# Sharing six PSUM banks as three for row scores and three for column scores, handed on tile by tile

## The reference, cut to what matters

```python
scores = jnp.einsum('bkgsd,bktd->bkgst', qh, kh) / scale
weights = jax.nn.softmax(scores, axis=-1)
out = jnp.einsum('bkgst,bktd->bkgsd', weights, vh)
...
x = x + jnp.tanh(g_xattn[0]) * xattn(_layernorm(x), ctx_512, ctx_512)
x = x + jnp.tanh(g_ffn[0]) * ffn(_layernorm(x), w_gate, w_up, w_down)
```

## Time and profile before

| | before |
|---|---|
| median of 3 runs | 472.99 us (472.53 to 473.21) |
| profiled execution | 472.9 us |
| its span in the trace | 471.1 us |
| TensorE busy in the span | 457.5 us (97%) |
| VectorE, ScalarE, GpSimd busy | 387.8, 291.7, 217.5 us |
| attention, about | 20 to 174 us |

### The profile page before, as it was taken

The page is one execution under the profiler, slowest core; times in us unless marked ns, Lnnn a source line. Parts: engine busy times, 40 slices in busy tenths (PEclk is TensorE's granted clock), DMA queues, the critical chain, the costliest instruction groups (busy, mean ns, idle before and its releaser), DMA issues.

```text
span 471.1 us, 8996 instructions
## 1 busy us (share of the span) xinstructions
PE 457.5 (97%) x3108; PEld 299.2 (64%) x3128; DVE 387.8 (82%) x715; ACT 291.7 (62%) x464; POOL 217.5 (46%) x335
## 2 busy tenths in 40 slices
PE   9999999999999989989999999999999999999997
PEld 8665656666566534468944479864469874479664
DVE  5879988788877659859998967999885999889891
ACT  3488886677778688877647417653616663657460
POOL 4355556989898464655006734203926300930000
PEclk9999999999999999999999999999999999999999
DMA  7999120121014041000100651100361110152086
GB/s 233 323 349 352 36 52 11 24 58 25 13 25 111 13 162 40 2 0 13 24 11 3 111 140 27 22 11 0 69 154 46 24 24 0 33 91 57 1 141 217
DMA packets 68183, 35.90 MB, mean 76 GB/s; under 512 B 50288, under 2 KB 62960, under 8 KB 68144
## 3 DMA queue, kind: packets, MB, share of 16 engines
q1 hardware_dynamic: 67408, 34.48, 28.8%
q10 hardware_dynamic: 736, 0.92, 0.6%
HBM read 19.26 MB, written 4.19 MB: 50 GB/s over the span
## 4 chain that ended last, share of the span: by engine, by line
PE 78%; DVE 9%; ACT 5%; issue 5%; DMA 1%; POOL 1%; DVEq 0%; SPq 0%; POOLq 0%; ACTq 0%
PE ps L872 16%; PE ps L623 10%; PE ps L926 9%; PE ps L949 9%; PE ps L605 8%; PE ps L666 6%; PE ps L683 4%; PE ps L938 2%; PE ps L940 2%; PE ps L815 2%; PE ps L585 2%; PE ps L725 2%; DVE y_split L1440 2%; ACT wst L1067 2%; PE ps L631 1%
## 5 line engine op out<-in xcount | busy, mean ns | idle before, releaser
L872 PE MATMUL ps<-wst 128*128 128x512 bf16 x499 | 111.7, 379 | 3.3 <-DVE wst L1460 2.1
L1297 DVE TENSOR_REDUCE reg<-ps 128x4 f32<-128x512 f32 x128 | 81.8, 683 | 24.9 <-PE ps L623 23.3
L872 PEld LDWEIGHTS ps<-wst 128*128 128x128 bf16 x512 | 49.2, 98 | 62.1 <-DVE wst L1460 4.1
L623 PE MATMUL ps<-reg 32*128 32x256 f32 x512 | 86.8, 400 | 0.5 <-DVE reg L1297 0.2
L569 POOL TENSOR_TENSOR reg_rest<-reg_rest,z_sc 128x1024 f32<-128x1024 f32 x24 | 47.4, 2010 | 84.7 <-DVE z_sc L1502 84.7
L1029 ACT ACTIVATE reg<-ps 128x1024 f32<-128x1024 f32 x64 | 65.6, 1025 | 33.0 <-PE ps L631 32.9
L1160 ACT ACTIVATE wst<-wst 128x512 f32<-128x512 f32 x64 | 40.0, 626 | 51.4 <-DVE wst L1460 51.0
L926 PE MATMUL ps<-had_f,wst 128*128 128x128 f32 x512 | 67.1, 276 | 1.1 <-DVE wst L1465 1.1
L926 PEld LDWEIGHTS ps<-had_f,wst 128*128 128x128 f32 x512 | 64.0, 191 | 4.4 <-DVE wst L1465 1.8
L605 PE MATMUL ps<-reg 32*128 32x512 f32 x232 | 65.2, 639 | 0.0
L623 PEld LDWEIGHTS ps<-reg 32*128 32x128 f32 x512 | 58.7, 184 | 6.0 <-issue 1.0
(11 more groups left out here) (172 smaller groups left out, 739.2 us busy)
## 6 DMA issues: line engine op xcount, KB each, us to landing
wst<-in_w SPq DMA_DIRECT2D x16, 512.0 KB, 8.6
reg<-in_w SPq DMA_DIRECT2D x8, 512.0 KB, 5.6
out<-x_all SPq DMA_DIRECT2D x16, 256.0 KB, 2.1
x_all<-in_x SPq DMA_DIRECT2D x3, 1024.0 KB, 9.5
reg<-in_v SPq DMA_DIRECT2D x4, 256.0 KB, 4.2
reg<-in_k_t SPq DMA_DIRECT2D x28, 32.0 KB, 2.7
x_all<-in_x ACTq DMA_DIRECT2D x1, 512.0 KB, 6.6
reg_rest<-reg SPq DMA_TRANSPOSE x20, 3.1
```

Of the source, the lines that this page charges most:

```text
L623: last = pe.matmul(ps[:, row_banks(r) + m, 256 * g:256 * g + 256], q_t[n % 4][strip(i), P * h:P * h + P], kpad[n // CHUNK % 2][strip(i), n ...
L872: last = pe.matmul(ps[:, banks[ob % n], :], tern_gu[:, ob // 2, m, j, P * (ob % 2):P * (ob % 2) + P], q1_t[:, j, :], start=(j == 0), stop= ...
L1297: dve.tensor_reduce(neg_max[n % 2][:, g:g + 2, i + m, :], ps[:, row_banks(r) + m, :].rearrange("p (g a t) -> p g a t", g=2, a=2), AX_X, AL ...
```

## The change

Rows get banks 0 to 2 and columns banks 3 to 5, each used in rotation by single tiles. A row tile waits for the third tile before it to be reduced, in place of the second; only in the first quarter on three banks (r = 7) does it wait as before. A column tile waits for the exponential of the third tile before it. `cols_done` and `exp_done` count tiles, not quarters: each mask product increments, and each exponential of 512 columns. All waits on these counts, on SP, TensorE and ScalarE, are restated in tiles. The six lone quarters keep their pairs of banks and their exponentials of 1,024 columns; their first pair waits for all exponentials before it. The first two column quarters both wait for 12 maxima, where the first waited for 10.

```diff
-        C_BANKS = 2
+        ROW_BANKS, COL_BANKS = 3, 3
+        TILES = 2 * QUARTERS
...
-        def column_bank(c):
+        def column_bank(c, m):
             if c < LONE:
-                return C_BANKS + 2 * (c % 2)
-            return (2, 0, 4)[(c - LONE) % 3]
-        def row_banks(r):
-            return 2 * (r % 3) if r < LEAD else 0
+                return ROW_BANKS + (2 * c + m) % COL_BANKS
+            return (2, 0, 4)[(c - LONE) % 3] + m
+        def row_bank(r, m):
+            if r < LEAD:
+                return 2 * (r % 3) + m
+            return (2 * (r - LEAD) + m) % ROW_BANKS
...
                 if exists(b):
-                    reach(pe, sem("exp_done"), c - 1)
                     if c < 2:
-                        pe.wait_ge(sem("max_done"), 2 * (5 + c))
+                        pe.wait_ge(sem("max_done"), 2 * 6)
                     for m, i in enumerate(own):
-                        pe.matmul(ps[:, bank + m, :], ...
+                        reach(pe, sem("exp_done"), 2 * c + m - COL_BANKS + 1)
+                        pe.matmul(ps[:, column_bank(c, m), :], ...
...
-                    past = r - 1 if r >= LEAD else r - 3
                     for m, i in enumerate(other):
-                        reach(pe, sem("max_done"), 2 * past + 1 + m)
+                        if r >= LEAD + 1:
+                            reach(pe, sem("max_done"), 2 * r + m - ROW_BANKS + 1)
+                        elif r == LEAD:
+                            pe.wait_ge(sem("max_done"), 2 * r + m - 1)
+                        else:
+                            reach(pe, sem("max_done"), 2 * (r - 3) + 1 + m)
...
                     for m, i in enumerate(own):
-                        last = pe.matmul(ps[:, bank + m, :], sel[strip(i), a, :], ...)
-                    last.then_inc(sem("cols_done"), 1)
+                        pe.matmul(ps[:, column_bank(c, m), :], sel[strip(i), a, :], ...
+                                  ).then_inc(sem("cols_done"), 1)
...
                 for k in range(2):
-                    pe.wait_ge(sem("exp_done"), c + k - (1 if c + k == LONE else 2))
+                    pe.wait_ge(sem("exp_done"), 2 * (c + k) - (0 if c + k == LONE else 4))
...
-                act.wait_ge(sem("cols_done"), c + 1)
                 reach(act, sem("pv_done"), 2 * n + j // 2 - 1)
-                bank = column_bank(c)
-                act.activation(probs[:, 2 * j:2 * j + 2, :], ps[:, bank:bank + 2, :], ACT.Exp,
-                               scale=D ** -0.5).then_inc(sem("exp_done"), 1)
+                if c < LONE:
+                    for m in range(2):
+                        act.wait_ge(sem("cols_done"), 2 * c + m + 1)
+                        act.activation(probs[:, 2 * j + m, :], ps[:, column_bank(c, m), :], ACT.Exp,
+                                       scale=D ** -0.5).then_inc(sem("exp_done"), 1)
+                else:
+                    act.wait_ge(sem("cols_done"), 2 * c + 2)
+                    bank = column_bank(c, 0)
+                    act.activation(probs[:, 2 * j:2 * j + 2, :], ps[:, bank:bank + 2, :], ACT.Exp,
+                                   scale=D ** -0.5).then_inc(sem("exp_done"), 2)
```

More of the change, by code:

```diff
@@ L313, in turn_maxima @@
                 sp.wait_ge(sem("ms"), 5 * n + 5)
-                sp.wait_ge(sem("cols_done"), QUARTERS * (n - 1))
+                sp.wait_ge(sem("cols_done"), TILES * (n - 1))
                 sp.dma_start_transpose(m_t[n % 2].rearrange("p (g q) -> p g q", g=G), m_parts).then_inc(sem(f"m_in{n % 2}"), 16)
             def more_keys(c):
-                sp.wait_ge(sem("cols_done"), QUARTERS * CHUNK * (c - 1))
+                sp.wait_ge(sem("cols_done"), TILES * CHUNK * (c - 1))
                 load_keys(c)
@@ L327, in _ @@
                 if b == 12:
-                    sp.wait_ge(sem("cols_done"), 3 * CHUNK * QUARTERS)
+                    sp.wait_ge(sem("cols_done"), 3 * CHUNK * TILES)
                     sp.wait_ge(sem("pv_done"), 2 * 3 * CHUNK)
@@ L335, in _ @@
                     turn_maxima(b + 1)
-            sp.wait_ge(sem("cols_done"), NB * QUARTERS)
+            sp.wait_ge(sem("cols_done"), NB * TILES)
             sp.wait_ge(sem("v_set"), NB // CHUNK)
@@ L598, in quarter @@
                 own, other = (2 * (j % 2), 2 * (j % 2) + 1), (2 * (k % 2), 2 * (k % 2) + 1)
-                a, bank = j // 2, column_bank(c)
+                a = j // 2
                 if exists(b):
-                    reach(pe, sem("exp_done"), c - 1)
                     if c < 2:
-                        pe.wait_ge(sem("max_done"), 2 * (5 + c))
+                        pe.wait_ge(sem("max_done"), 2 * 6)
                     for m, i in enumerate(own):
-                        pe.matmul(ps[:, bank + m, :], kpad[b // CHUNK % 2][strip(i), b % CHUNK, a, :], q_t[b % 4][strip(i), :],
+                        reach(pe, sem("exp_done"), 2 * c + m - COL_BANKS + 1)
+                        pe.matmul(ps[:, column_bank(c, m), :], kpad[b // CHUNK % 2][strip(i), b % CHUNK, a, :], q_t[b % 4][strip(i), :],
                                   start=True, stop=False)
@@ L610, in quarter @@
                         for m, i in enumerate(own):
-                            last = pe.matmul(ps[:, bank + m, :], sel[strip(i), a, :], m_t[0][strip(i), :], start=False, stop=True)
-                        last.then_inc(sem("cols_done"), 1)
+                            pe.matmul(ps[:, column_bank(c, m), :], sel[strip(i), a, :], m_t[0][strip(i), :], start=False, stop=True
+                                      ).then_inc(sem("cols_done"), 1)
                 if exists(n):
@@ L617, in quarter @@
                             pe.wait_ge(sem(f"k_in{n // CHUNK % 2}"), 16 * NKV * (n // CHUNK // 2 + 1))
-                    past = r - 1 if r >= LEAD else r - 3
                     for m, i in enumerate(other):
-                        reach(pe, sem("max_done"), 2 * past + 1 + m)
+                        if r >= LEAD + 1:
[4 more added lines that the diff above has]
+                            reach(pe, sem("max_done"), 2 * (r - 3) + 1 + m)
                         for g in range(2):
                             h = 2 * (k // 2) + g
-                            last = pe.matmul(ps[:, row_banks(r) + m, 256 * g:256 * g + 256], q_t[n % 4][strip(i), P * h:P * h + P],
+                            last = pe.matmul(ps[:, row_bank(r, m), 256 * g:256 * g + 256], q_t[n % 4][strip(i), P * h:P * h + P],
                                              kpad[n // CHUNK % 2][strip(i), n % CHUNK, :, :].rearrange("p a t -> p (a t)"),
@@ L630, in quarter @@
                     for m, i in enumerate(own):
-                        last = pe.matmul(ps[:, bank + m, :], sel[strip(i), a, :], m_t[b % 2][strip(i), :], start=False, stop=True)
-                    last.then_inc(sem("cols_done"), 1)
+                        pe.matmul(ps[:, column_bank(c, m), :], sel[strip(i), a, :], m_t[b % 2][strip(i), :], start=False, stop=True
+                                  ).then_inc(sem("cols_done"), 1)
             def column_pair(b, j):
@@ L646, in column_pair @@
                     for m, i in enumerate((2 * k, 2 * k + 1)):
-                        last = pe.matmul(ps[:, column_bank(c + k) + m, :], sel[strip(i), a, :], m_t[b % 2][strip(i), :],
+                        last = pe.matmul(ps[:, column_bank(c + k, m), :], sel[strip(i), a, :], m_t[b % 2][strip(i), :],
                                          start=False, stop=True)
-                    last.then_inc(sem("cols_done"), 1)
+                    last.then_inc(sem("cols_done"), 2)
             def weigh(n, kvh):
@@ L656, in weigh @@
                     pe.wait_ge(sem("v_set"), n // CHUNK + 1)
-                pe.wait_ge(sem("exp_done"), QUARTERS * n + 2 * kvh + 2)
+                pe.wait_ge(sem("exp_done"), TILES * n + 4 * kvh + 4)
                 reach(pe, sem("oev_done"), 2 * n + kvh)
@@ L889, in gate_up @@
                         turn_out(NB - 1, 1)
-                        pe.wait_ge(sem("exp_done"), QUARTERS * NB)
+                        pe.wait_ge(sem("exp_done"), TILES * NB)
                         early_groups()
@@ L977, in project_last @@
                     product(LAST_TO[tb], tb, q2_last, 0, NC).then_inc(sem("d_done"), 1)
-            pe.wait_ge(sem("exp_done"), QUARTERS * NB - 1)
+            pe.wait_ge(sem("exp_done"), TILES * NB - 2)
             pe.wait_ge(sem("max_done"), 2 * QUARTERS * NB)
@@ L1042, in copy_max @@
                 act.wait_ge(sem("tm_done"), n + 1)
-                reach(act, sem("cols_done"), QUARTERS * (n - 1))
+                reach(act, sem("cols_done"), TILES * (n - 1))
                 act.copy(m_t[n % 2], M_BANK).then_inc(sem("mt_done"), 1)
@@ L1049, in copy_queries @@
                 act.wait_ge(sem("tq_done"), n + 1)
-                reach(act, sem("cols_done"), QUARTERS * (n - 3))
+                reach(act, sem("cols_done"), TILES * (n - 3))
                 act.copy(q_t[n % 4], O_BANK).then_inc(sem("qt_done"), 1)
```

4 lines of the change are left out of this document (2 added, 2 removed).

## The result

The changed kernel takes 469.98 us, the median of 20 runs (469.62 to 477.1), against 472.45 us for the kernel before in the same series (472.12 to 480.7, also 20 runs): a ratio of 0.9964, interval 0.9948 to 0.9979. A second series, with twelve runs of it, gave 470.07 us and 0.993 (0.9905 to 0.9956). The forecast was 469.5 us. The profile read here is therefore that of the second series: span 468.1 us, 469.93 us in all, where before had 471.1 and 472.9.

What follows compares the result with a forecast made beforehand. The bound was taken as TensorE's order, stretched by waits for VectorE. Gains 0.5 + 0.7 + 0.4 + 0.8 + 1.6 less 0.6 lost make 3.4 us, giving 469.5 us; range 466.6 to 472.4.

Steps and rivals of the forecast that it cites:

- The bound: Attention, 20 to 166 us: TensorE's order, stretched by waits for VectorE that its busy share hides; ceiling 11.5 us.
- The exponential's wait: Ten quarters, mostly first ones from step 5: second column product 0.16 us late, so 1.75 becomes about 1.43.
- Steps 1 to 4: After step 1's first quarter: ceiling 1.2 us less three second-quarter stalls of 0.17, 0.7 gained.
- The start: Step 0 and the first quarter of step 1: 0.5 us gained, between 0 and the ceiling 2.5.
- Step 5: Step 5 of the attention: 0.6 us less one exponential wait of 0.16, 0.4 gained.
- Steps 11 to 14: After the first quarter of step 11: 2.2 us less four exponential waits of 0.16, 1.6 gained.
- The cap: Steps 6 to 11: GpSimd, with little idle time, limits the gain to 0.8 of 5.0 us.
- Rival 1: Steps 6 to 11: GpSimd caps nothing, 3.9 us gained in place of 0.8, total 466.4 us; chance 0.1.
- The lone pair: End of attention: first lone pair newly waits for the last quarter's exponential, 0.6 us lost.
- Rival 2: Exponential halves without overlap take most of the gain back; 1 to 2 us remains, 471.5 us; chance 0.2.
- Rival 3: No change: VectorE late by one tile more, exponential waits take the rest; 472.8 us; chance 0.1.
- Rival 4: Slower: second column waits for the exponential's half at each quarter's head, if about 0.88 us; 475.2 us; chance 0.1.

Runs made afterwards that it cites:

- e_row_two: The changed kernel, but a row tile again waits for the second tile before it to be reduced; 473.98 us, ratio 1.0017.
- e_halves_before: The kernel before the change, with only each exponential of 1,024 columns split into two of 512; 472.82 us, ratio 1.0002.
- e_one_inc: The changed kernel with one increment of 2 on the second mask product in place of one on each; 470.12 us, ratio 0.9958.
- e_light_after: The changed kernel with GpSimd's shifts of the first 14 halves of weights made over 128 of 1,024 columns; 468.66 us, ratio 0.9893.
- v_even_end: As v_even, but ScalarE normalises batches 12 and 14 at the ends of steps 8 and 10, behind a sign; 467.8 us, ratio 0.9867.
- v_moved: The changed kernel with e_lone's wait and query normalisations of batches 10, 11, 13 moved from GpSimd to ScalarE at ends of steps 6, 7, 9; 468.85 us.
- e_lone: The changed kernel, but of the first lone pair only the product overwriting bank 3 waits, only for the tile there; 469.34 us, ratio 0.9937.
- e_rows_first: The changed kernel with the second column product issued behind the row products in place of ahead of them; 470.4 us, ratio 0.9932.
- v_even: The changed kernel with e_lone's wait and normalisations of batches 10, 12, 14 on ScalarE, 12 and 14 inside steps 9 and 11; 468.17 us.

## Why the prediction was right, and where it was off

**The bound.** That TensorE's busy time hides waits for VectorE, and that a third row bank ends most of them, holds: third quarters went from 1.38 to 1.27, as foretold, and e_row_two puts the bank at 4.2 us. Eight quarters, not seven, had a length of their own; the sum of 11.5 is right.

**The exponential's wait.** Right in kind and too small: 0.21 in place of 0.16, so first quarters take 1.48 and not 1.43. The halves are nearly what I took, 0.597 us against 0.59 and 0.49 apart against 0.485. What moved is their start: 1.43 after the quarter's (71.92, 73.35), where I kept the 1.38 of the kernel before. In both kernels the mask products end 1.34 after the quarter's start. The split alone does not delay the exponential (1.38 in e_halves_before), nor does the second increment (1.44 with one, in e_one_inc). What is left is how ScalarE waits: its wait for the columns now stands directly before the exponential, behind that for the weighing, where it stood ahead of it. That was not tried. Of the ten places nine take 1.47 to 1.49 in the trace, and the first quarter of step 8 takes 1.40. The Trainium skill (ScalarE: Activation LUTs, "What ACT_TABLE_LOAD costs") gives, as estimates by its formula, a half 613 ns and the pair 0.09 over a whole one; the trace shows 597 ns, and 1.08 against 1.02 for the pair, 0.06.

**Steps 1 to 4** was the term that failed: 0.7 foretold, 0.31 measured. I let three second quarters stall by 0.17. In the trace four do, that of step 1 too, each by 0.21:

```profile
39.95 0.91 PE L608 MATMUL ps<-reg 32*128 32x512 f32 x2
...
41.43 0.66 PE L690 MATMUL ps<-ident_f,reg 128*128 128x128 f32 x4
```

1.48 from one to the other, where my text had 1.27 + 0.17 = 1.44. Four times 0.21 is 0.84, which takes 1.2 down to 0.36.

**The start** gave 0.70 in place of 0.5, inside its bounds of 0 and 2.5. **Step 5** gave 0.36 (0.4). **Steps 11 to 14**: four times 0.21 in place of 0.16 takes 1.6 down to 1.4; 1.32 was measured.

**The cap** was the term that carried most: 0.8 of 5.0, and 0.88 was measured. I had counted what GpSimd has idle between the addition at 76.63 and the transposition at 129.83, 53.20 us apart; in the change the same two, at 75.18 and 127.50, are 52.32 apart, which is 0.88 less. The waits at L741 (0.64, 0.97, 0.90, where I had said half a microsecond), e_light_after and v_even_end show GpSimd's work as the cause. What the count by idle time left out is that VectorE's finish comes within 0.1 us of the end of GpSimd's work ahead of the addition: e_light_after and v_moved show that less load there brings nothing. That the two limits fall together, so that a count of the load gave the right size, is luck. Of the 5.0 the forecast was right to leave most. Rival 1, by which nothing caps, would have had 3.9 here.

**The lone pair**: foretold 0.6 lost, measured 0.64: the pair started 0.80 later, 2.66 behind its quarter in place of 1.86, and 0.16 came back behind it. That the wait is the cause of the 0.80 is shown by e_lone, whose pair starts 1.86 behind its quarter again; how much of it reaches the end is known to some 0.3 only.

**The rivals.** Rival 2 needed halves without overlap; they overlap, and e_halves_before costs 0.2. Rival 3 needed VectorE to be late by one more tile; first quarters at 1.48 say no, though a row wait does remain in the second quarter of step 6 (1.75 to 1.41). Rival 4 needed a half of 0.88 us; it takes 0.597. It has a grain of truth: without the third row bank the change is 1.4 slower than the kernel before.

**The sum.** 3.4 was foretold for the span and 3.0 came: +0.2 at the start, -0.4 in steps 1 to 4, -0.3 in the last steps, the others within 0.1. That 0.4 is the whole distance between the forecast of 469.5 and the profiled 469.93. That the median of 469.98 lies as near is luck in part: the forecast started from a median before of 472.99 (less 3.4, it is 469.6 and not 469.5), and the series gave 472.45, so a gain that was 0.7 to 0.9 smaller in the medians than foretold moved the time by only 0.4 to 0.5.

## What to carry to other kernels

Where products lie side by side on the array, a busy share of 100% says nothing of TensorE's waits (145.8 of 146 us held 11.5 us of them here): take a stretch that waits for nothing as the ruler, lay it on each repetition, and the sum of what is over is the ceiling of a change. Then ask of each released wait which chain takes its place, and walk that chain from its trigger to its use: only relief inside it pays, and here moving three normalisations of which one lay inside brought 0.5 us, and three that all did 1.6. A counter that is changed from pairs to tiles wants every wait on it worked out anew; the one at the lone pair, kept a tile too cautious, cost about 0.6 (0.3 by the spans of the two traces).

## What was not expected of the hardware

In the profiled execution of the first series TensorE's granted clock was at its lower level, 1.2 GHz, for a while at the start. Two stretches of it (columns as in the earlier trace rows):

```profile
15.00:20.00 5.00, 5.00 (x24) 2.98 (x23) 4.96 (x10) 0.76 (x1) 1.32 (x6) 0.67 1.10 351
20.00:25.00 5.00, 5.00 (x35) 4.60 (x35) 1.19 (x2) 2.33 (x3) 1.04 (x3) 0.65 1.10 349
```

From 18 to 20 us the clock is 0.50, which is that level; it is still full up to 16 us and full again from 24. The first quarter starts at 23.79 us in place of 20.03, and from there on the two traces of the change agree to 0.1 us. In order of time, what lies ahead:

```profile
12.21 0.69 DVE L1297 BATCH_NORM_STATS2 few<-x_all 128x6 f32<-128x512 f32 x1 [1.24 <-DMA x_all<-in_x]
...
13.84 1.63 PE L630 MATMUL ps<-reg 32*128 32x256 f32 x8 [0.66 <-DVE reg L1310]
```

The second series' trace, with the full clock throughout:

```profile
10.78 0.69 DVE L1297 BATCH_NORM_STATS2 few<-x_all 128x6 f32<-128x512 f32 x1
...
13.30 1.14 PE L630 MATMUL ps<-reg 32*128 32x256 f32 x8 [0.23 <-ACT reg L1064]
```

The input landed later (the statistics start at 12.21 in place of 10.78), TensorE then stood idle for 0.66 us in place of 0.23, and behind that the clock fell. The other profiles agree: in the four with the lower clock (this one, e_one_inc, e_rows_first, v_even) the idle time at this place is 0.66, 0.97, 0.89 and 1.01, and the first quarter starts at 23.79, 24.24, 23.94 and 25.68 us; in the nine with the full clock it is 0.23 each time, and the first quarter starts at 19.8 to 20.1. All of this lies ahead of the first quarter with columns, where the change alters nothing. Executions without a profile show only their mean clock, so where it fell in them isn't known. Which executions have it varies from series to series: 6 of 20 of the change in the first, none of 12 in the second; 3 of 35, 4 of 23 and 3 of 17 of the kernel before. Over all runs whose clock is on record it is 20 of 105 for kernels with the change and 14 of 99 for those without. Whether the change has any part in it is not settled by these counts, and what decides over the landing was not tried.

That the normalisations cost ScalarE's chain 0.4 us less at the end of a step (v_even_end) than inside the next (v_even) is measured and not explained. By the traces 0.3 of it lies in the second quarters of steps 9 and 11, from whose starts to the thirds' it is 2.98 and 3.00 in v_even and 2.84 and 2.82 in v_even_end.
